# ScalarE centres the rows of the second normalisation, and VectorE adds attention one slot sooner

## The reference

```
v  = layernorm of x over channels                      (per pixel)
ca = sigmoid(mlp(mean over pixels) + mlp(max over pixels))   (per image, channel)
v  = v * ca
sa = sigmoid(conv7x7([mean over channels, max over channels] of v))
x  = x + v * sa
t  = x as tokens (pixels) of 512 channels
n  = (t - mean(t)) / sqrt(var(t) + 1e-5)
h  = gelu(bitlinear(n, w1))        # w1: 2048 x 512
x  = t + bitlinear(h, w2)          # w2: 512 x 2048
bitlinear(a, w): w rounded to -1, 0, 1 times 1/rms; a rounded to 255 levels of its row's largest magnitude
```

## Time and profile before

| | us |
|---|---|
| median of 3 runs | 310.25 (309.97 to 312.55) |
| the profiled execution's own time | 312.61 |
| its span, first to last instruction | 310.9 |
| bodies 1 to 4, convolution to convolution | 30.3 each |
| body 5 (no `turn_x`) | 31.3 |

### The profile page before, as it was taken

The page is one execution under the profiler, slowest core; times in us unless marked ns, Lnnn a source line. Parts: engine busy times, 40 slices in busy tenths (PEclk is TensorE's granted clock), DMA queues, the critical chain, the costliest instruction groups (busy, mean ns, idle before and its releaser), DMA issues.

```text
span 310.9 us, 5833 instructions
## 1 busy us (share of the span) xinstructions
PE 270.1 (87%) x1834; PEld 155.4 (50%) x1834; DVE 253.3 (81%) x558; ACT 217.2 (70%) x442; POOL 162.8 (52%) x261
## 2 busy tenths in 40 slices
PE   2665659686999999999999999999999987999974
PEld 2453544463546555645564556555555544444431
DVE  0756979989699989998999899899989997888410
ACT  2277488568586878687868777887678856676831
POOL 9503374515955395548564855576556663346410
PEclk9999775859699999999999999999999999799998
DMA  5899500001356048514941294339324723063593
GB/s 135 301 380 422 182 1 2 0 0 37 33 139 101 1 70 207 134 21 49 239 100 37 54 249 72 35 70 253 54 40 71 160 40 67 12 174 73 75 210 102
DMA packets 71078, 34.20 MB, mean 110 GB/s; under 512 B 52040, under 2 KB 68424, under 8 KB 70536
## 3 DMA queue, kind: packets, MB, share of 16 engines
q1 hardware_dynamic: 69384, 32.78, 44.4%
q10 hardware_dynamic: 1664, 1.05, 1.2%
HBM read 14.94 MB, written 6.29 MB: 68 GB/s over the span
## 4 chain that ended last, share of the span: by engine, by line
PE 39%; DVE 37%; issue 10%; ACT 7%; DMA 3%; POOL 2%; SPq 1%; ACTq 0%; DVEq 0%
PE ps_o L1188 12%; PE ps_h L1177 7%; DVE amax L875 7%; PE ps_t L1177 6%; DVE t L848 5%; PE small L1153 3%; PE front L1107 3%; DVE pv L816 3%; DVE st L850 3%; DVE amax L861 3%; DVE cen L860 2%; PE ps_t L1219 2%; DVE w_room L918 2%; PE front L1197 2%; DVE res L892 2%
## 5 line engine op out<-in xcount | busy, mean ns | idle before, releaser
L1188 PE MATMUL ps_o<-w2T,hq 128*128 128x512 f16 x384 | 92.6, 380 | 1.3 <-DMA hq<-w_raw 1.3
L483 POOL TENSOR_SCALAR w_room<-w_room,q 128x1024 f32<-128x1024 f32 x48 | 57.2, 1202 | 50.6 <-DVE q L885 50.1
L875 DVE TENSOR_REDUCE amax<-w_room 128x1 f32<-128x1024 f32 (+1 forms) x48 | 57.2, 1208 | 2.3 <-ACT w_room L542 2.2
L1177 PE MATMUL ps_h<-w1T,xq 128*128 128x512 f16 x208 | 55.9, 415 | 1.2 <-ACT xq L542 1.1
L1188 PEld LDWEIGHTS ps_o<-w2T,hq 128*128 128x128 f16 x384 | 36.3, 98 | 36.0 <-DMA hq<-w_raw 1.8
L542 ACT ACTIVATE w_raw<-w_room 128x1024 f16<-128x1024 f16 x48 | 50.4, 1052 | 0.6 <-POOL w_room L483 0.6
L542 ACT ACTIVATE w_room<-ps_h,s 128x512 f32<-128x512 f32 x52 | 35.0, 688 | 15.2 <-PE ps_h L1177 14.1
L1177 PE MATMUL ps_t<-w1T,xq 128*128 128x512 f16 x176 | 42.7, 386 | 0.0
L542 ACT ACTIVATE w_room<-ps_t,s 128x512 f32<-128x512 f32 x44 | 30.2, 687 | 8.2 <-PE ps_t L1177 5.6
L1177 PEld LDWEIGHTS ps_h<-w1T,xq 128*128 128x128 f16 x208 | 20.4, 105 | 24.7 <-issue 5.5
L542 ACT ACTIVATE junk_m<-front 128x192 bf16<-128x192 f32 x64 | 20.6, 332 | 16.0 <-DVE pooled L787 16.0
(11 more groups left out here) (126 smaller groups left out, 456.2 us busy)
## 6 DMA issues: line engine op xcount, KB each, us to landing
out<-w_room SPq DMA_DIRECT2D x16, 384.0 KB, 3.3
x_in<-in_x SPq DMA_DIRECT2D x14, 384.0 KB, 5.1
w_room<-in_L_ffn_w SPq DMA_DIRECT2D x4, 1024.0 KB, 8.9
w_raw<-in_L_ffn_w SPq DMA_DIRECT2D x4, 1024.0 KB, 12.1
x_in<-in_x ACTq DMA_DIRECT2D x2, 384.0 KB, 4.0
hq<-w_raw SPq DMA_TRANSPOSE x48, 3.1
fc_raw<-in_L_conv_fc_w ACTq DMA_DIRECT2D x2, 128.0 KB, 4.3
taps_rev<-in_L_conv_sa_w SPq DMA_DIRECT2D x2, 0.2 KB
```

What stands on the lines that cost most here:

```text
L483: pool.tensor_scalar(part, part, q2[tile.par][:, 0:1], MAGIC, ALU.mult, ALU.add).then_inc(g_rounded, 1)
L875: chain.mark(dve.tensor_reduce(amax2[:, i:i + 1], w1_room[:, first + i * F // 2:first + (i + 1) * F // 2 + i], AX.X, ALU.max, apply_absolu ...
L1177: last = pe.matmul(banks[b], xq[tile.pair.par][:, tile.s, k, :], w1T[:, k, b * 512:(b + 1) * 512], start=(k == 0), stop=(k == NC - 1))
L1188: last = pe.matmul(ps_o[:, :], hq[tile.par][:, k, :], w2T[:, k, :], start=(k == 0), stop=(k == NF - 1))
```

## The change

ScalarE gets a function of its own that centres a tile, as mean minus value (`Identity` with scale −1 and the mean as bias). VectorE's `centre` becomes `limit`, which waits for it and does the rest; the sign is undone in q1 (times −127). In the loop VectorE's list is written anew: `add_attention` of a tile comes a slot sooner, the second with a `token_max` between its first two instructions; `add_ffn(pair,2)` moves from the start of the next body to the end of this one; the first two scalings of channels come ahead of `hidden_max(nxt,1,0)`. GpSimd does two of the `rstd2` sooner. TensorE's and SyncE's lists stay the same.

```diff
@@ -222,6 +222,7 @@
         rs2_ready = sem("rs2_ready")
         q1_ready = sem("q1_ready")
         cen_rounded = sem("cen_rounded")
+        cen_ready = sem("cen_ready")
         xq_turned = sem("xq_turned")
         xq_ready = sem("xq_ready")
         h_done = sem("h_done")
@@ -514,12 +515,12 @@
                     round_g(Tile(pair, 1), (1,))
                 if normalise:
                     round_x(Tile(nxt, 0))
+                    rstd2(Tile(nxt, 1))
                 round_g(Tile(pair, 2))
                 if normalise:
-                    rstd2(Tile(nxt, 1))
                     round_x(Tile(nxt, 1))
+                    rstd2(Tile(nxt, 2))
                     round_g(Tile(nxt, 0))
-                    rstd2(Tile(nxt, 2))
                     round_x(Tile(nxt, 2))
                 if turn:
                     normalise1(fresh, 0, 1)
@@ -581,6 +582,13 @@
             def gate_tokens(pair):
                 wait(act, conv_sum_ready, pair.at(1, 1))
                 copy(sg_tanh[pair.par][:, :], conv_sum[:, :], sg_tanh_ready, ACT.Tanh, scale=0.5)
+
+            def centre(tile):
+
+                wait(act, stats2_ready, tile.at(1, 1))
+                wait(act, xq_turned, tile.at(1, -1))
+                copy(cen[tile.par][:, :], t[tile.pair.par][:, tile.s, :], cen_ready, ACT.Identity, scale=-1.0,
+                     bias=mv2[tile.par][:, 0:1])
 
             def copy_xq(tile, bank):
                 wait(act, xq_turned, tile.at(1, 1))
@@ -656,6 +664,7 @@
             gate_tokens(pair0)
             copy_weights(0, (4, 5, 6, 7))
             squares(1, w2_raw, w2_loaded, (0,))
+            centre(Tile(pair0, 0))
             copy_xq(Tile(pair0, 0), 0)
             token_mean(pair1, 0, 1)
             squares(1, w2_raw, w2_loaded, (1,))
@@ -667,6 +676,7 @@
             token_mean(pair1, 3, 1)
             copy_weights(1, (2, 3))
             gate_channels(pair1)
+            centre(Tile(pair0, 1))
             copy_weights(1, (4,))
             copy_xq(Tile(pair0, 1), 0)
             copy_caT(pair1)
@@ -677,6 +687,7 @@
             gelu(Tile(pair0, 1), None, h_start, (1,))
             sum_channels(Tile(pair1, 2))
             gelu(Tile(pair0, 1), None, h_start, (2, 3))
+            centre(Tile(pair0, 2))
             pack_g(Tile(pair0, 0), 0)
             pack_g(Tile(pair0, 0), 1)
             copy_x(Tile(pair2, 0), 1)
@@ -687,7 +698,10 @@
             def body(pair, attend, normalise, turn):
                 nxt, att, fresh = pair.plus(1), pair.plus(2), pair.plus(3)
 
-                gelu(Tile(pair, 2), nxt if normalise else None)
+                gelu(Tile(pair, 2), nxt if normalise else None, blocks=(0, 1, 2))
+                if normalise:
+                    centre(Tile(nxt, 0))
+                gelu(Tile(pair, 2), blocks=(3,))
                 pack_g(Tile(pair, 1), 0)
                 if pair.c > 0:
                     copy_out(Tile(pair.plus(-1), 2), OUT_BANK[0])
@@ -702,7 +716,9 @@
                     token_mean(att, 2, V1_BANK[2])
 
                 if normalise:
-                    gelu(Tile(nxt, 0))
+                    gelu(Tile(nxt, 0), blocks=(0,))
+                    centre(Tile(nxt, 1))
+                    gelu(Tile(nxt, 0), blocks=(1, 2, 3))
                 pack_g(Tile(pair, 2), 0)
                 copy_out(Tile(pair, 0), OUT_BANK[1])
                 if attend:
@@ -717,6 +733,7 @@
                     copy_x(Tile(fresh, 1), X_BANK[1])
 
                 if normalise:
+                    centre(Tile(nxt, 2))
                     gelu(Tile(nxt, 1), blocks=(0, 1))
                 if attend:
                     copy_caT(att)
@@ -838,33 +855,33 @@
                 wait(dve, sg_tanh_ready, pair.at(1, 1))
                 link(dve.tensor_scalar(sg[pair.par][:, :], sg_tanh[pair.par][:, :], 0.5, 0.5, ALU.mult, ALU.add))
 
-            def add_attention(tile):
+            def add_attention(tile, between=None):
 
                 par, s = tile.pair.par, tile.s
                 t_tile = t[par][:, s, :]
                 wait(dve, scaled, tile.at(1, 1))
                 wait(dve, xt_ready, tile.at(1, 1))
                 wait(dve, res_ready, tile.at(1, 1 - 2 * NT))
-                link(dve.scalar_tensor_tensor(t_tile, pv[par][:, s, :], sg[par][:, s:s + 1],
-                                              xt[par][:, s, :], ALU.mult, ALU.add))
+                chain.mark(dve.scalar_tensor_tensor(t_tile, pv[par][:, s, :], sg[par][:, s:s + 1],
+                                                    xt[par][:, s, :], ALU.mult, ALU.add))
+                if between:
+                    token_max(*between)
+                chain.wait()
                 link(dve.bn_stats(st2[:, :], t_tile))
                 wait(dve, rs2_ready, tile.at(1, -1))
                 dve.bn_aggr(mv2[tile.par][:, :], st2[:, :]).then_inc(stats2_ready, 1)
 
-            def centre(tile):
-
-                par, s = tile.pair.par, tile.s
-                t_tile, c = t[par][:, s, :], cen[tile.par]
-                wait(dve, stats2_ready, tile.at(1, 1))
-                wait(dve, xq_turned, tile.at(1, -1))
-                link(dve.tensor_scalar(c[:, :], t_tile, mv2[tile.par][:, 0:1], None, ALU.subtract))
+            def limit(tile):
+
+                c = cen[tile.par]
+                wait(dve, cen_ready, tile.at(1, 1))
                 link(dve.tensor_reduce(amax1[:, :], c[:, :], AX.X, ALU.max, apply_absolute_value=True))
                 wait(dve, rs2_ready, tile.at(1, 1))
                 r = rs2[tile.par][:, 0:1]
                 link(dve.tensor_scalar(lim1[:, :], amax1[:, :], r, EPS, ALU.mult, ALU.max))
                 link(dve.reciprocal(rec1[:, :], lim1[:, :]))
                 wait(dve, cen_rounded, tile.at(1, -1))
-                dve.tensor_scalar(q1[tile.par][:, :], rec1[:, :], r, 127.0, ALU.mult, ALU.mult).then_inc(q1_ready, 1)
+                dve.tensor_scalar(q1[tile.par][:, :], rec1[:, :], r, -127.0, ALU.mult, ALU.mult).then_inc(q1_ready, 1)
 
             def hidden_max(tile, i):
 
@@ -986,7 +1003,7 @@
             copy_weights(0, (3,))
             token_gate(pair0)
             add_attention(Tile(pair0, 0))
-            centre(Tile(pair0, 0))
+            limit(Tile(pair0, 0))
             token_max(pair1, 0, 1)
             squares(1, w2_raw, w2_loaded)
             weight_sum(1)
@@ -1001,7 +1018,7 @@
             token_max(pair1, 3, 1)
             copy_weights(1, (1,))
             hidden(pair1)
-            centre(Tile(pair0, 1))
+            limit(Tile(pair0, 1))
             split_gate(pair1)
             hidden_max(Tile(pair0, 0), 0)
             copy_weights(1, (5,))
@@ -1011,7 +1028,7 @@
             hidden_scale(Tile(pair0, 0))
             scale_channels(Tile(pair1, 2), 1)
             add_attention(Tile(pair0, 2))
-            centre(Tile(pair0, 2))
+            limit(Tile(pair0, 2))
             hidden_max(Tile(pair0, 1), 0)
             hidden_max(Tile(pair0, 1), 1)
             split_stats(pair1)
@@ -1023,58 +1040,56 @@
             def body(pair, attend, normalise, turn):
                 nxt, att, fresh = pair.plus(1), pair.plus(2), pair.plus(3)
 
-                if pair.c > 0:
-                    add_ffn(Tile(pair.plus(-1), 2))
                 if normalise:
                     token_gate(nxt)
                     add_attention(Tile(nxt, 0))
-                    centre(Tile(nxt, 0))
+                hidden_max(Tile(pair, 2), 0)
+                if normalise:
+                    limit(Tile(nxt, 0))
                 if attend:
                     token_max(att, 0, V1_BANK[0])
-                hidden_max(Tile(pair, 2), 0)
                 if attend:
                     token_max(att, 1, V1_BANK[1])
                 hidden_max(Tile(pair, 2), 1)
+                if normalise:
+                    add_attention(Tile(nxt, 1), (att, 2, V1_BANK[2]) if attend else None)
                 hidden_scale(Tile(pair, 2))
-                if attend:
-                    token_max(att, 2, V1_BANK[2])
 
                 add_ffn(Tile(pair, 0))
                 if normalise:
-                    add_attention(Tile(nxt, 1))
-                    centre(Tile(nxt, 1))
+                    limit(Tile(nxt, 1))
+                    hidden_max(Tile(nxt, 0), 0)
                 if attend:
                     token_max(att, 3, V1_BANK[3])
                 if normalise:
-                    hidden_max(Tile(nxt, 0), 0)
                     hidden_max(Tile(nxt, 0), 1)
                 if attend:
                     hidden(att)
                 if normalise:
+                    add_attention(Tile(nxt, 2))
                     hidden_scale(Tile(nxt, 0))
 
                 add_ffn(Tile(pair, 1))
-                if normalise:
-                    add_attention(Tile(nxt, 2))
                 if attend:
                     split_gate(att)
                 if normalise:
-                    centre(Tile(nxt, 2))
-                    hidden_max(Tile(nxt, 1), 0)
+                    limit(Tile(nxt, 2))
                 if attend:
```

(14 more changed lines are left out.)

## The result

The changed kernel takes **333.8 us** (median of 4 runs, 333.45 to 336.25); the kernel before took 310.62 beside it. The ratio is 1.074, interval 1.0693 to 1.0787. The prediction was slower, with 320.0 and a range up to 326.5: the sign is right, the size is not.

A forecast was written before the change was run, and what follows sets the result against it. It took hand-over waits between nearly full VectorE and TensorE as the bound. To 310.25 us it added prologue +5.7, five bodies +3.0, body 5 −1.0 and one clock fall 1.7: 319.7, rounded to 320.0 us; range 313.5 to 326.5.

The forecast's parts named there:

- What bounds the kernel: Steady loop: VectorE and TensorE both nearly full, so hand-over waits count; TensorE's floor 28.85 us a body.
- I take 0.75 for each: VectorE's loop: the two long add_attention fall to 0.75 us each, 1.2 us less; work per body falls to about 25.5.
- The hand-over from spread to scaling: Before the convolution: VectorE idles about 1 us, then the moved hidden_max lengthens first scaling to convolution from 5.47 to 6.6.
- The wait at `turn_ca`, taken off the sum: TensorE in the loop: its 0.37 us wait for VectorE at turn_ca goes, so it comes to spread_ca at 23.6.
- the forecast 30.85: Length of a loop body in us: 23.6 + 0.4 + 6.6 = 30.6, plus TensorE's 0.25 lateness from ScalarE.
- What ScalarE adds in the loop: Centring of (nxt,0) between GELUs delays ScalarE 0.3 and TensorE 0.25 us through the copy of xq; the other two cost nothing.
- The prologue: Centrings queued on ScalarE delay the first three tiles by 3.1, 1.5 and 1.1 us: +5.7, bounds +4 and +6.5.
- Body 5: Loop body without turn_x: earlier split_gate starts the first scaling 1.2 us sooner, convolution 6.6 after it: −1.0 us.
- The clock: TensorE idles about 1.6 us before each convolution; a clock fall costs 1.7 us, zero to five falls, one likeliest.
- the rounding of 0.56 a body to 0.6: Five loop bodies with all parts, each taken as about 0.6 us longer than before: +3.0 us.
- VectorE was the bound, and freeing it pays: Rival: moved hidden_max costs nothing, loop bodies reach 28.85, 8.4 us less; 302 with the prologue's waits hidden; chance 0.04.

The follow-up runs named there:

- experiment 12: Kernel before, with only split_stats moved ahead of hidden_scale(nxt,1); VectorE still does all centring: 303.48 us, ratio 0.9737.
- experiment 2: Changed kernel with split_gate moved ahead of hidden_scale(nxt,0) and add_ffn(pair,1) in VectorE's list: 323.86 us, ratio 1.0399.
- experiment 11: Changed kernel with hidden_scale(nxt,0), which starts GpSimd's round_g, moved behind split_gate; the split stays behind add_ffn(pair,1): 321.99 us, ratio 1.031.
- experiment 1: Changed kernel with hidden_max(nxt,1,0) back ahead of the three channel scalings in VectorE's loop: 332.12 us, ratio 1.0658.
- experiment 6: Changed kernel's ScalarE centring, but VectorE's and GpSimd's loop lists in the order of before, limit in the old centring's place: 321.37 us, ratio 1.0294.
- experiment 7: Changed kernel with split_gate ahead of hidden_scale(nxt,0), hidden_max(nxt,1,0) ahead of the first scaling, channel_stats between second and third: 316.03 us, ratio 1.0131.
- experiment 3: Changed kernel with ScalarE's three prologue centrings each moved ahead of one longer piece of its list: 330.38 us, ratio 1.0598.
- experiment 5: Changed kernel's new VectorE and GpSimd order alone: VectorE centres every tile itself, ScalarE's list is that of the kernel before: 327.26 us, ratio 1.0486.
- experiment 8: As experiment 7, but VectorE centres the prologue's three tiles and ScalarE centres in the loop only: 309.9 us, ratio 0.9924.
- experiment 9: As experiment 8, with split_stats also moved ahead of hidden_scale(nxt,1): 304.34 us, ratio 0.9749.
- experiment 10: Changed kernel with only hidden_max(nxt,1,0) ahead of the first scaling and channel_stats between second and third; split_gate not moved: 323.43 us, ratio 1.0367.
- experiment 4: Changed kernel with seven unread 512-column matmuls added on TensorE ahead of each loop convolution: 328.48 us, ratio 1.0546.

## Why the prediction was right or wrong

**What bounds the kernel: right.** The sum gave TensorE a floor of 28.85 us a body; experiment 12 has bodies of 29.09 in which TensorE doesn't idle, so the floor is nearer that. What counts is the hand-overs. What I read too lightly is the earlier trace rows: the 0.37 us before the convolution were on the path in every body, and one small swap takes out 1.2 us.

**"I take 0.75 for each": the number is right, the conclusion is the step that failed.** All `add_attention` of the loop take 0.75. But I took the contention with GpSimd off the sum because the `add_attention` had left the neighbourhood of `round_g`, and didn't ask who had moved in. `hidden_scale(nxt,0)` lets `round_g` start, and behind it now stand `add_ffn(pair,1)` and `split_gate`, which TensorE waits for. Size: 1.10 us a body (experiments 2 and 11). VectorE's work in a body is 27.6 us, not 25.5, and the two stretched subtractions are 1.8 of that difference.

**The hand-over from spread to scaling: right.** Forecast 6.6 us from the first scaling to the convolution; measured 6.74 (178.06 to 184.80). VectorE idles 1.14 before it, forecast about 1. TensorE idles 1.63 before the convolution, forecast 1.6. Experiment 1 corrects the picture: the cover that `hidden_max` gave was for two waits, and only with `channel_stats` back between the scalings does the end of the list give its 1.27.

**The wait at `turn_ca`, taken off the sum: wrong,** as a consequence of the failed step: 0.92 us of idle TensorE instead of none. Of the 1.38 us by which the body exceeds the forecast 30.85, the split is 1.10. The rest, 0.28, is left in experiment 2 too: the first scaling starts 24.39 us after the convolution where the sum had 24.25, and the next convolution 6.74 behind it where it had 6.6.

**What ScalarE adds in the loop: small, but priced too low and put in the wrong place.** I had 0.25 us through the copy of xq. The trace shows it at `turn_v1`, through `copy_out`: that TensorE instruction starts 7.38 us after the convolution instead of 7.02, and the `ffn_in` of (nxt,0) 10.02 instead of 9.63. The operation takes 0.61 start to start and 0.72 in itself, where I assumed 0.52; less the 0.22 that was covered, 0.39. Experiment 6 has the same lateness at `turn_v1`, and its body is still only 0.1 longer than before, since VectorE's work falls there from 28.3 to 25.8. The centrings of (nxt,1) and (nxt,2) add nothing, as forecast: `caT` is ready 0.6 us ahead of the first spread (experiment 7). The Trainium skill ("ScalarE: Activation LUTs", section "What ACT_TABLE_LOAD costs") gives more for an operation whose bias is a pointer to one value a row than for one with constants, and an overlap of about 93 ns between neighbours. The trace agrees with that page: 0.72 long against 0.58 to 0.63 for the copies and channel sums, and 0.11 of overlap. I had read only those shorter rows. No further table load came, as forecast.

**The prologue: the sum is right, its shares less so.** +5.7 forecast, +5.8 measured. The squares of w2 start at 48.15 against 48.55. Up to the squares, to the second and to the third maximum of a centred row, the loss grows by 2.7, 3.1 and 0.6 us (forecast 3.1, 1.5 and 1.1), and 0.6 are regained by the convolution. Experiment 3 gives back 3.7; experiments 5 and 8, with VectorE centring, give back all.

**Body 5: the number is right by luck.** −1.0 forecast; +0.85 measured, with one fall of the clock of 1.7 behind the convolution ahead of it, so −0.85 without. In experiment 3, which has the same loop, this body runs at full clock and takes 30.49 against 31.32 before. But its first scaling comes 0.7 us later than before, not 1.2 sooner, as the failed step stands here too: the split is stretched, and TensorE waits 1.83 us at `turn_ca`. And the convolution follows the scaling after 5.0 us, not 6.6, because `split_stats`, which I left at 2.1 us, takes 0.4: in the changed kernel it starts at 284.36, just ahead of `round_g` (284.51), where before it started 0.12 behind it. Two errors cancel. The changed kernel's rows, beside the earlier trace rows:

```profile
276.29 1.06 DVE L827 TENSOR_TENSOR ca_row<-ca_row 128x8 f32<-128x8 f32 x1
...
284.56 0.17 DVE L847 TENSOR_TENSOR ch_stat<-ch_stat 128x6 f32<-128x6 f32 x1
```

**The clock: mechanism right, count wrong, the second term that was mis-sized.** I took one of five further falls; there were four, and the fall after body 5's convolution, which the kernel before has, is gone. In full, where I had 1.7 us: bodies 1, 3, 4 and 5 lose 1.5 to 1.7 us each behind a fall, and the tail gains 1.5. Body 0 is another 1.3 longer than the other bodies explain; it starts at a granted 0.50, before at 0.62, and I count it here, though no run shows it apart. Together 6.3 us. The forecast idle time was right to 0.03 us. With this same idle time of 1.63 us a fall followed 4 times in 5 in the changed kernel and in experiments 3 and 5, but 2 times in 5 in experiments 2 and 11, in one profiled execution of each. What decides between them stays open: no run here tells it apart.

Sum in spans: 9.4 forecast, 9.2 without the rounding of 0.56 a body to 0.6; 6.9 more for five bodies at 1.38; 4.6 for the clock; 0.3 for prologue and body 5 together: 21.0, against 20.9 measured.

**The rivals.** "VectorE was the bound, and freeing it pays" was rightly rare as the change stood. But with both hand-overs repaired the body is 29.87. Experiments 9 and 12 show that even then the freed time buys nothing that a two-line swap doesn't: 29.33 with ScalarE centring, 29.1 without. The first still has TensorE's wait for `copy_out`, the second has none.

## What to carry to other kernels

When a VectorE instruction is moved away from GpSimd's work, look at what stands there now; a step of 8 elements on the path can cost as much as one of 512. Put the small steps that another engine waits for ahead of the instruction that releases GpSimd, and take out the smallest wait of the bounding engine first: it may be cheaper to remove than a whole operation is to move. Between steps that each wait for another engine, every filler covers a particular wait, so price its place, not only its length.

## What the runs showed of the hardware that was not expected

- **Tiny VectorE instructions can last as long as their neighbour on GpSimd.** 8 elements a row: 0.17 us alone, 1.06 beside `round_g`, ending each with one of its halves. The Trainium skill ("SBUF — State Buffer", section "Who interferes with whom") says that a VectorE instruction with two SBUF inputs contends with a GpSimd one that reads SBUF, and that the pair of ports they share is an exclusive lock. The trace agrees, with 174.53 and 175.62 against ends near 174.50 and 175.61. Whether two of them meet hangs on less than 0.1 us: the subtraction at 173.47 starts 0.08 us behind `round_g` and takes 1.06, the one at 284.56 starts 0.05 behind it and takes 0.17. What decides at that distance no run shows.
- **One input is no protection.** In experiment 5 the first step of `split_gate`, a `tensor_scalar` with one tensor input, met `round_g` (132.55, 2.21) and took 1.01 us instead of 0.17. The second subtraction, which starts when `round_g` is over, is back at 0.17:

```profile
132.69 1.01 DVE L821 TENSOR_SCALAR ca_row<-ca_tanh 128x8 f32<-128x8 f32 x1
133.74 1.05 DVE L823 TENSOR_TENSOR ca_row<-ca_row 128x8 f32<-128x8 f32 x1
134.82 0.17 DVE L824 TENSOR_TENSOR ca_row<-ca_row 128x8 f32<-128x8 f32 x1
```

- **The clock falls often after 1.63 us of idle TensorE, and never did after 0.37.** 16 of 25 such convolutions of bodies 0 to 4 (changed kernel, experiments 2, 3, 5 and 11) were followed by a lower granted clock, 2 of 5 after 1.15 us (experiment 1), none of 25 after 0.37 (the kernel before, experiments 6, 7, 8 and 10), and none of 5 after 0.12 (experiment 4, with fillers). When it falls, the next 5.1 us are granted 0.67 to 0.73, a part of them at 1.2 GHz instead of 2.4.
